# Node tiles of a graph network moved from one gather stage into the stage before it

## The reference

```python
x = _layernorm(x + _L0_gnn_ref(x, proj_cosim, W_ffn, b_ffn, src, dst))
x = _layernorm(x + _L1_gnn_ref(x, edge_attr_2, W_fc, W_attn, ..., src, dst))
x = _layernorm(x + _L2_gnn_ref(x, edge_index, W, att_src, att_dst, bias))
x = _layernorm(x + _L3_gnn_ref(x, edge_index, W1, b1, W2, b2))
```

## Time and profile before

| what | us |
|---|---|
| runs shown | 2577.59, 2573.97, 2572.82 (median 2573.97) |
| the profiled execution, its own time | 2577.51 |
| its span (first to last instruction) | 2575.7 |
| first gather stage, from its first gather to the next stage's first | 601.74 to 886.68 |
| second gather stage, to the first operation of the next | 886.68 to 1219.14 |
| VectorE busy in the span | 1867.6 (73%) |
| GpSimd busy | 1423.4 (55%) |
| TensorE, ScalarE busy | 1392.9 (54%), 791.9 (31%) |

### The profile page before, as it was taken

One profiled execution on the slowest core, in us unless ns is written; L12 is line 12 of the kernel. 1 busy time (PEld: TensorE's weight loads), 2 busy tenths in 40 slices (PEclk: granted clock), 3 DMA queues, 4 the chain that ended last, 5 costly groups with the idle time before them and its releaser, 6 DMA issues. The chain is left out here.

```text
span 2575.7 us, 25825 instructions
## 1 busy us (share of the span) xinstructions
PE 1392.9 (54%) x5738; PEld 832.2 (32%) x5738; DVE 1867.6 (73%) x3900; ACT 791.9 (31%) x1636; POOL 1423.4 (55%) x1382
## 2 busy tenths in 40 slices
PE   1433444444666588887466577634888543333231
PEld 1332333331333354443233455421333221212120
DVE  3877777875767589998688699977888675455542
ACT  1222222222545355554122355531222110101010
POOL 6777777735777576662000577730000277777776
PEclk9656555555877699999688899976888666566666
DMA  5433333431111233332011244420000011101010
GB/s 176 119 110 108 110 104 98 119 91 33 52 44 49 58 102 106 108 105 74 20 39 39 87 128 127 127 78 16 31 27 27 28 23 23 25 23 24 22 22 13
DMA packets 120400, 174.79 MB, mean 68 GB/s; under 512 B 36128, under 2 KB 42382, under 8 KB 120340
## 3 DMA queue, kind: packets, MB, share of 16 engines
q1 hardware_dynamic: 74836, 129.98, 15.0%
q0 software_dynamic: 43904, 43.81, 8.6%
q10 hardware_dynamic: 1600, 0.33, 0.1%
HBM read 88.48 MB, written 86.74 MB: 68 GB/s over the span
## 5 line engine op out<-in xcount | busy, mean ns | idle before, releaser
L461 POOL DMA_INDIRECT GA<-table,look_i x588 | 608.0, 1034 | 493.5 <-PEq L1473 213.0
L467 PE MATMUL P<-ident,GA 128*128 128x128 f32 x500 | 105.3, 348 | 411.6 <-DMA GB<-in_x,dst_i 198.9
L491 PE MATMUL P<-center,work 128*128 128x128 f32 x800 | 152.1, 352 | 210.9 <-DVE work L1697 174.2
L266 POOL DMA_INDIRECT GA<-in_x,src_i x196 | 210.6, 1074 | 83.5 <-issue 70.8
L1637 POOL DMA_INDIRECT out_x<-work,seg_i x196 | 205.0, 1046 | 59.8 <-issue 59.5
L1629 POOL DMA_INDIRECT GA<-table,look_i x196 | 200.2, 1022 | 59.8 <-issue 59.4
L266 POOL DMA_INDIRECT GB<-in_x,dst_i x196 | 196.9, 1004 | 59.7 <-issue 59.7
L509 ACT ACTIVATE work<-P 128x512 f32<-128x512 f32 x100 | 59.7, 597 | 518.6 <-PE P L491 518.1
L491 PEld LDWEIGHTS P<-center,work 128*128 128x128 f32 x800 | 135.9, 257 | 242.2 <-issue 113.1
L467 PEld LDWEIGHTS P<-ident,GA 128*128 128x128 f32 x500 | 71.1, 176 | 441.7 <-issue 222.3
L610 PE MATMUL P<-center,work 128*128 128x128 f32 x984 | 160.6, 313 | 91.1 <-ACT work L653 67.4
(11 more groups left out here) (332 smaller groups left out, 3448.9 us busy)
## 6 DMA issues: line engine op xcount, KB each, us to landing
table<-work SPq DMA_DIRECT2D x175, 256.0 KB, 2.4
XN<-in_x SPq DMA_DIRECT2D x98, 256.0 KB, 2.7
out_x<-work SPq DMA_DIRECT2D x98, 256.0 KB, 2.4
GA<-table,look_i POOLq DMA_INDIRECT x784, 2.4
XN<-in_src_pad SPq DMA_DIRECT2D x13, 512.0 KB
cols<-in_dst_pad SPq DMA_DIRECT2D x50, 128.5 KB, 4.7
table<-XN SPq DMA_DIRECT2D x1, 6400.0 KB
src_wide<-in_src_pad SPq DMA_DIRECT2D x12, 512.0 KB, 5.4
```

The lines of the kernel that those rows point to most:

```text
L266: pool.indirect_dma_start(buf[:, s % 2, j * D:(j + 1) * D], None, a["x"], bass.IndirectOffsetOnAxis(ap=look[:, s * 8 + j:s * 8 + j + 1], a ...
L461: pool.indirect_dma_start(GA[:, par, j * D:(j + 1) * D], None, table_k, bass.IndirectOffsetOnAxis(ap=look[:, s * 8 + j:s * 8 + j + 1], axis=0)
L467: ins = pe.transpose(dst[:, q * 128:(q + 1) * 128], src[:, q * 128:(q + 1) * 128], ident[:, :])
L491: ins = pe.matmul(norm_bank(par, far)[:, q * 128:(q + 1) * 128], W[par][4][:, q * 128:(q + 1) * 128], center[:, :], start=True, stop=True)
```

## The change

In the first gather stage both parities now share one gate bank (P[1]) and one back bank (P[3]). That frees P[5] and P[7], called NA and NB. In them the stage does one node tile beside each edge tile s: node tile 2s+1, spread over three further slots. Its load goes into XN in slot s, its transposes into NA in slot s+1, its products into NA and NB and its first normalisation in slot s+2, its second and the store from GB in slot s+3. The second gather stage is told `even=True` and leaves out the odd node tiles. So the same 50 node tiles are done, 25 in each stage. The core of the diff:

```diff
+        def back_pe_shared(pe, S, T, s, par, k):
+            yield 0
+            pe.wait_ge(T("emb"), k)
+            pe.wait_ge(S(f"kept{1 - par}"), k + par)
+            transpose4(pe, P[3], W[par][6]).then_inc(T("x_fm"), 1)
...
+        def only(base, *stages, even=False):
 
             def of_node(stage):
-                return lambda T, n, par, k: stage(T, n, par, k) if is_node(n, base) else None
+                return lambda T, n, par, k: stage(T, n, par, k) if is_node(n, base) and not (even and par) else None
             return [stage and of_node(stage) for stage in stages]
...
+        NX, NV = ([g[:, par, :] for par in range(2)] for g in (XN, GB))
+        NA, NB = P[5][:, :], P[7][:, :]
+        def tile_before(par, k):
+            return 1 - par, k - 1 + par
...
-                    dve.tensor_scalar(W[par][2], P[4 * par + 1][:, :], -5.0, 5.0, A.max, A.min).then_inc(T("clipped"), 1)
+                    dve.tensor_scalar(W[par][2], P[1][:, :], -5.0, 5.0, A.max, A.min).then_inc(T("clipped"), 1)
...
+                def node_first(T, s, par, k):
+                    yield 3
+                    dve.wait_ge(T("node_sq1"), k)
+                    dve.tensor_reduce(sm(par, 3), rows(NX[par]), AX, A.add).then_inc(T("node_ss1"), 1)
+                    yield 5
+                    dve.wait_ge(T("node_sd1"), k)
+                    dve.reciprocal(sm(par, 4), sm(par, 4)).then_inc(T("node_r1"), 1)
+                    dve.wait_ge(T("node_r1"), k)
+                    dve.tensor_tensor(rows(NV[par]), rows(NB), per_row(sm(par, 4)), A.mult).then_inc(T("node_y0"), 1)
+                    dve.wait_ge(T("node_y0"), k)
+                    dve.tensor_tensor(rows(NV[par]), rows(NV[par]), bias_row[:, :].rearrange("p (o f) -> p o f", o=1).to_broadcast([128, 8, D]),
+                                      A.add).then_inc(T("node_y"), 1)
...
+                def node_second(T, s, par, k):
+                    yield 1
+                    dve.wait_ge(T("node_sq2"), k)
+                    dve.tensor_reduce(sm(par, 5), rows(W[par][5]), AX, A.add).then_inc(T("node_ss2"), 1)
+                    yield 3
+                    dve.wait_ge(T("node_sd2"), k)
+                    dve.reciprocal(sm(par, 6), sm(par, 6)).then_inc(T("node_r2"), 1)
+                    dve.wait_ge(T("node_r2"), k)
+                    dve.tensor_tensor(rows(NV[par]), rows(NV[par]), per_row(sm(par, 6)), A.mult).then_inc(T("node_out"), 1)
                 keeping(dve, S0)
-                pipelined(dve, S0, gate, sums, partial(norm_dve, dve), partial(back_dve, dve))
+                pipelined(dve, S0, gate, sums, together(partial(norm_dve, dve), node_first),
+                          together(partial(back_dve, dve, bank=3), node_second))
...
-                    bank = P[4 * par + 1][:, :]
+                    bank = P[1][:, :]
                     yield 1
                     pe.wait_ge(T("product"), k)
+                    if not (isinstance(s, int) and s == 0):
+                        older, turn = tile_before(par, k)
+                        pe.wait_ge(S0(f"clipped{older}"), turn)
                     pe.matmul(bank, proj[:, :], W[par][0], start=True, stop=True).then_inc(T("cos"), 1)
...
+                def node_turn(T, s, par, k):
+                    yield 4
+                    pe.wait_ge(T("node_x"), 16 * k)
+                    older, turn = tile_before(par, k)
+                    if not (isinstance(s, int) and s == 0):
+                        pe.wait_ge(S0(f"node_sq1{older}"), turn)
+                    transpose4(pe, NA, NX[par]).then_inc(T("node_xt"), 1)
+                def node_dense(T, s, par, k):
+                    yield 1
+                    older, turn = tile_before(par, k)
+                    pe.wait_ge(T("node_vt"), k)
+                    if not (isinstance(s, int) and s == 0):
+                        pe.wait_ge(S0(f"node_y0{older}"), turn)
+                    for w, p in ((center, NA), (chain, NB)):
+                        for q in range(4):
+                            ins = pe.matmul(p[:, q * 128:(q + 1) * 128], NV[par][:, q * 128:(q + 1) * 128], w[:, :], start=True, stop=True)
+                    ins.then_inc(T("node_mm"), 1)
+                pipelined(pe, S0, gate, together(sums, node_turn), together(partial(norm_pe, pe), node_dense), partial(back_pe_shared, pe, S0))
...
+                def node_start(T, s, par, k):
+                    yield 6
+                    act.wait_ge(T("node_xt"), k)
+                    act.wait_ge(T("node_stored"), 16 * k)
+                    act.activation(NV[par], NA, ACT.Identity, bias=relub).then_inc(T("node_vt"), 1)
+                def node_first(T, s, par, k):
+                    yield 2
+                    act.wait_ge(T("node_mm"), k)
+                    act.activation(NX[par], NA, ACT.Square).then_inc(T("node_sq1"), 1)
+                    yield 4
+                    act.wait_ge(T("node_ss1"), k)
+                    act.activation(sm(par, 4), sm(par, 3), ACT.Sqrt, scale=(1.0 + EPS) / D, bias=eps_2).then_inc(T("node_sd1"), 1)
+                def node_second(T, s, par, k):
+                    yield 0
+                    act.wait_ge(T("node_y"), k)
+                    act.wait_ge(T("variance"), k)
+                    act.activation(W[par][5], NV[par], ACT.Square).then_inc(T("node_sq2"), 1)
+                    yield 2
+                    act.wait_ge(T("node_ss2"), k)
+                    act.activation(sm(par, 6), sm(par, 5), ACT.Sqrt, scale=(1.0 + EPS) / D, bias=eps_2).then_inc(T("node_sd2"), 1)
+                pipelined(act, S0, gate, together(sums, node_start), together(partial(norm_act, act), node_first), node_second)
...
+                def node_load(T, s, par, k):
+                    yield 0
+                    if not (isinstance(k, int) and k == 1):
+                        sp.wait_ge(T("node_ss1"), k - 1)
+                    sp.dma_start(NX[par], rows_of(a["x"], (2 * s + 1) * SE)).then_inc(T("node_x"), 16)
+                def node_store(T, s, par, k):
+                    yield 4
+                    sp.wait_ge(T("node_out"), k)
+                    sp.dma_start(rows_of(out, (2 * s + 1) * SE), NV[par]).then_inc(T("node_stored"), 16)
                 storing(sp, S0)
-                pipelined(sp, S0, None, None, lambda T, s, par, k: store_table(sp, T, table[1], s, par, k, 6))
+                for par in range(2):
+                    sp.sem_inc(S0(f"node_stored{par}"), 16)
+                pipelined(sp, S0, node_load, None, lambda T, s, par, k: store_table(sp, T, table[1], s, par, k, 6), node_store)
...
-                pass_back(dve, S1, lambda stage: nodes_vector(dve, S1, 0, (2, stage), (3, cube(0)), (4, cube(1))))
+                pass_back(dve, S1, lambda stage: nodes_vector(dve, S1, 0, (2, stage), (3, cube(0)), (4, cube(1)), even=True))
...
```

More of the change, by code:

```diff
@@ L701, in first_of, with nodes_sync @@
             return N - SE if is_last(n, base) else (n + base) * SE
-        def only(base, *stages):
+        def only(base, *stages, even=False):
             def of_node(stage):
-                return lambda T, n, par, k: stage(T, n, par, k) if is_node(n, base) else None
+                return lambda T, n, par, k: stage(T, n, par, k) if is_node(n, base) and not (even and par) else None
             return [stage and of_node(stage) for stage in stages]
-        def nodes_sync(sp, S, base, *owns):
+        def nodes_sync(sp, S, base, *owns, even=False):
             def load(T, n, par, k):
@@ L1285, in logits @@
                     act.activation(ROW[par][0:4, :], own_bank(par)[0:4, :], ACT.Copy).then_inc(S1(f"row{par}"), 1)
-                nodes_scalar(act, S1, 0, (2, states), (3, square(0)), (4, square(1)), (5, logits))
+                nodes_scalar(act, S1, 0, (2, states), (3, square(0)), (4, square(1)), (5, logits), even=True)
             @block.sync
```

30 lines of the change are left out of this document (15 added, 15 removed).

## The result

| | us |
|---|---|
| before, 13 runs | median 2575.95 (2570.76 to 2583.84) |
| after, 13 runs | median 2569.33 (2564.28 to 2575.75) |
| ratio | 0.9972, 95% interval 0.996 to 0.9983 |

The change makes the kernel about 7 us faster. Forecast were 20 us. The profiled execution took 2570.3 us (span 2568.5 against 2575.7), which is the same 7 us, so its trace can be used to say where they come from.

A forecast was written before the change was run, and what follows sets the result against it. VectorE was taken to bound the second stage, the gathers' pace the first. Terms: -48 (second stage) + 20 (first, steady) + 8 (first, end) = -20 us; against the median of 2574.0, 2554 us, range 2540 to 2579.

The forecast's parts named there:

- first stage, steady: First gather stage with one node per tile added: VectorE becomes the bound at 11.6 us per tile, 20 us more.
- first stage, end: Last gated product to the next stage's first gather: grows from 15.1 us to about 23, 8 us more.
- second stage, first to last gather: Second gather stage without odd nodes: gathers take the first stage's 262.7 us in place of 291.6.
- second stage, last gather to last turning: Second stage, after the last gather starts: its own 0.94 us and a landing of some 2.4, together 3.3.
- second stage, tail: Last tile's transposes to the next stage: 19 us, between 18 and 21.6, against 21.6 today.
- The loop through SyncE: First stage: node store behind the load, landing, GB freed for ScalarE, L1154, next gated product; 10.7 to 11.6 us.
- signs of being wrong: Products 12.5 us or more apart; first-stage VectorE waiting for L1225 or TensorE; L1154 waiting behind the store; second-stage buffer waits.
- 8.3 + L: First stage, time per tile of the loop through SyncE, L being the node store's landing; 10.7 us with L 2.4.
- Half clock in the first stage: Rival: TensorE at half clock in the first stage, tile 13.6 us with today's mix, total 2598 us; chance 0.11.
- Late store: Rival: first stage's node store lands late, L of 5 us, loop 13.3 us, total 2592 us; chance 0.03.
- The last rival: Second stage held at about 11.7 us by its own order of steps, 22 of 48 us given back, 2576; chance 0.04.
- Work only moved: Rival: VectorE's total stays; first stage loses 47 us at 12.43 per tile, second gains 48, total 2573; chance 0.12.

The follow-up runs named there:

- store_first: Changed kernel with the node's load issued behind the node's store on SyncE in the first stage; first stage 306.8 us, ratio 0.9938 to the kernel before.

## Why the prediction was wrong

| step, as predicted | predicted | measured |
|---|---|---|
| first stage, up to tile 2 | 0 | -1.6 |
| first stage, steady | +20 (11.6 us per tile) | +25 (11.8) |
| first stage, end | +8 | +6.4 |
| second stage, first to last gather | -28.9 (262.7) | -23.8 (267.8) |
| second stage, last gather to last turning | 3.3 | 6.6 |
| second stage, tail | 19 | 20.0 |
| second stage in all | -48 (45 to 51) | -38.1 |
| sum with what lies around | -20 | -7.2 |

With their decimals the terms of the forecast make -19.0 (-47.5 + 20.5 + 8), 12 us more than the -7.2 measured: 9.4 in the second stage, 1.2 in the first, 1.2 in what lies around.

**The first stage was right in its mechanism, and in its sum partly by luck.** VectorE filled up as forecast (222.39 of 240 us from 640 to 880), with 11.8 us per tile in the forecast's 11.2 to 12.2. The next stage's first gather came at 914.90 where 915 was named. By stage 29.7 us were added where 28 were summed, but three misses cancel in that: the steady part came 4.4 us over its 20.5, the start 1.6 and the end 1.6 under. The end, 914.90 - 893.37 = 21.5, is 6.4 over the 15.1 of the earlier trace rows (its terms make 22.4 only if the 1 us of waits comes on top of the 5.7). VectorE's own need was put at 11.2 and is 11.4. The loop through SyncE was named as what could sit in the last 0.4 us, and `store_first` shows that it does: L1154 did wait for ScalarE behind the store, one of the signs of being wrong. The store landed after 3.0 us, not the 2.4 of the earlier trace rows. The estimate for two DMAs in line by the fit of the Trainium skill (DMA: Bandwidth & Descriptors, Anatomy of one DMA), 3.2 us, was the nearer one. With 3.0 the loop as I worked it, 8.3 + L, is 11.3; the tile shown above takes 11.75, because SyncE issues the store 6.8 us in and not 6.3.

**The second stage was the wrong step**, the sentence "The first gather to the last then takes what it takes in the first stage, 262.7 us". It took 267.8, 5.1 us of the 9.4. Its support was that "one gather lasts no longer", from busy sums of 202.48 and 204.59 in the earlier trace rows. These sums hide that in the second stage few gathers met a scan, at a high price each, while GpSimd stood still for the rest of them. With the waiting gone the sum is 208.01. The gathers that start in a scan cost 21.2 us over their 0.94 each, where those of the first stage cost 12.5, and the others 3.1 less than there; that makes the 5.5 us between 208.01 and 202.48. The third stage's 279 us, my witness for the pace, has the same backward scans, met as often, but at a later point of the scan and so for 12.6 us. The direction of the scan is not what costs.

**The stage's end** was off by 4.3. The turning came 6.6 us after the last gather and not 3.3: it does not follow the landing, as I had it, but the copy that frees its bank, and then the node's products ahead of it in TensorE's order. The tail came to 20.0 and not 19.

**The rivals.** Half clock in the first stage: wrong, the granted clock rose to 0.90 with more work in the stage, as the third stage's 0.95 had said. TensorE was busy 207.92 of 314 us and itself waited for VectorE and ScalarE. It waited 35.6 us for L476 between 640 and 880 us, in nearly every tile and 2.0 us at the longest, and was granted 0.93 there. So the falling back in every tile of which the Trainium skill (TensorE: Matmul & The Clock Gate, HAM oscillation) tells did not come. The kernel in that section waits for a DMA in each tile, and longer than TensorE does here; I had applied it without this condition. Late store: right as a mechanism, wrong in size, L is 3.0 and not 5, and it costs 0.35 us per tile. The last rival, a second stage that does not come down to the gathers' pace as the first stage has it, was given 4 in 100 and comes nearest to what happened: 9.4 of its 22 us, 5.1 of them by slower gathers and not by the order of steps, 4.3 at the stage's end. "Work only moved" gives nearly the time (2573 against the 2569 measured) but not the mechanism: it put 47 us on the first stage and took 48 from the second; measured were 29.7 and 38.1.

## What to carry to other kernels

A wait that is taken away exposes whatever it covered on the same engine: before taking a pace from another stage, look at single operations beside each other engine's long ones, how many meet and at which point (the distribution, not the busy sum), since here 28 gathers that start inside a scan became 47. Between a load and a store on one queue, put first what somebody waits for: that single number took 8 us off the stage, about as much as the whole move brought. And means per tile do not balance two engines when the heavy and the light tiles alternate and only two buffers lie between them.

## What the runs showed of the hardware

- A gather issued by GpSimd takes 0.94 us alone and up to 1.9 when it starts inside a segment scan of 64x512 on VectorE (1.28 us): 241 of the 243 gathers counted above ended 0.75 to 0.83 us after the scan, forward or backward, and 101 that started up to 0.8 us ahead of it took 0.94 to 0.96. With the scan replaced by one product of the same operands the mean falls from 1.061 to 0.983. Leaving out 50 DMAs of 256 KB in the stage changed it by 0.004.
- A node tile's store of 256 KB right behind a load of the same size on SyncE's queue landed after 3.0 us (median of 25), the other node tiles' stores of this kernel after 2.1, and the same 25 after 2.1 in `store_first`, with the load behind them.
- The clock granted to TensorE in the first stage was 0.78 between 640 and 860 us before, 0.93 with the node tiles, and 0.98 with the store ahead, at 144.96, 152.13 and 149.53 us busy of 220. In the last two the work is the same and only its gaps differ.
